# A transformer block for eight batches on one core: the loop over the batches written out, score stacks loaded in halves, maxima taken in the other order

## What is computed

```python
h = layernorm(x) * (1 + ca) + sa
q, k, v = (h @ w.T + (h @ a.T @ b.T) / 16 for w, a, b in three_sets)   # 16 heads of 16
attn = softmax(causal(q @ k.T / 4)) @ v
x = x + ga * lora_linear(attn, wo, ao, bo)
h = layernorm(x) * (1 + cb) + sb
w = top-2 softmax weights of 4 experts, from h @ Wg.T + bg
hid_e = relu(h @ Wi.T + lora_e(h))                                     # 1024 wide, e = 0..3
x = x + gb * sum_e w_e * (hid_e @ Wo.T)
```

## Time and profile of the kernel before

| | |
|---|---|
| time, median of 3 runs | 2154.45 us (2153.02 to 2154.53) |
| span of the profiled execution | 2145.5 us |
| PE busy | 1892.0 us (88%) |
| DVE busy | 1199.8 us (56%) |
| ACT busy | 938.8 us (44%) |
| POOL busy | 529.7 us (25%) |
| mean granted clock of PE | 0.959 |

### The profile page before, as it was taken

The page is one execution under the profiler, slowest core; times in us unless marked ns, Lnnn a source line. Parts: engine busy times, 40 slices in busy tenths (PEclk is TensorE's granted clock), DMA queues, the critical chain, the costliest instruction groups (busy, mean ns, idle before and its releaser), DMA issues.

```text
span 2145.5 us, 36829 instructions
## 1 busy us (share of the span) xinstructions
PE 1892.0 (88%) x11124; PEld 980.5 (46%) x11124; DVE 1199.8 (56%) x2697; ACT 938.8 (44%) x1701; POOL 529.7 (25%) x823
## 2 busy tenths in 40 slices
PE   8687888999889989899889998899898998798858
PEld 5233343455435454354534555354543545344435
DVE  3755567555665557655575556655576554755132
ACT  2254444544444544544444444444445443544421
POOL 3111122322222212223223222222122232132223
PEclk9889989999999999999999999999999999999979
DMA  5523333121433222232331214332222323210100
GB/s 170 80 50 60 60 57 78 22 63 23 80 60 67 33 39 77 31 70 32 65 79 20 62 24 81 60 67 33 36 70 41 70 31 65 31 26 16 35 0 20
DMA packets 72349, 111.82 MB, mean 52 GB/s; under 512 B 13940, under 2 KB 41680, under 8 KB 72152
## 3 DMA queue, kind: packets, MB, share of 16 engines
q1 hardware_dynamic: 72136, 109.31, 27.3%
q10 hardware_dynamic: 16, 0.02, 0.0%
HBM read 75.20 MB, written 33.57 MB: 51 GB/s over the span
## 4 chain that ended last, share of the span: by engine, by line
PE 61%; DVE 14%; DMA 8%; issue 7%; SPq 5%; ACT 4%; POOL 0%; DVEq 0%; POOLq 0%; ACTq 0%
PE mxs L747 11%; PE ov L776 9%; PE st L761 9%; PE dense L856 8%; DMA k_st<-k_parts_scratch 8%; PE dense L841 5%; DVE negm L1147 4%; PE dense L867 4%; PE dense L791 4%; SPq L577 4%; PE dense L833 3%; PE dense L733 3%; PE mxs L751 2%; SPq L581 1%; DVE stats L1018 1%
## 5 line engine op out<-in xcount | busy, mean ns | idle before, releaser
L915 ACT ACTIVATE probs<-st 128x512 f32<-128x512 f32 (+1 forms) x1216 | 666.9, 576 | 651.2 <-PE st L761 613.2
L747 PE MATMUL mxs<-k_st,q_st 96*128 96x512 bf16 (+3 forms) x1536 | 463.4, 333 | 54.6 <-DMA k_st<-k_parts_scratch 48.2
L1147 DVE TENSOR_REDUCE negm<-mxs 128x1 f32<-128x512 f32 (+4 forms) x736 | 416.1, 613 | 147.8 <-PE mxs L751 147.4
L761 PE MATMUL st<-q_st,k_st 98*128 98x512 bf16 (+3 forms) x1536 | 453.0, 335 | 38.9 <-issue 24.3
L1147 DVE TENSOR_REDUCE negm_left<-mxs 128x1 f32<-128x512 f32 x512 | 330.0, 684 | 168.0 <-PE mxs L747 165.5
L776 PE MATMUL ov<-probs,v_g 128*32 128x512 f32 (+3 forms) x3072 | 333.5, 506 | 22.7 <-POOL probs L634 21.9
L747 PEld LDWEIGHTS mxs<-k_st,q_st 96*128 96x128 bf16 x1536 | 149.0, 98 | 333.9 <-issue 101.7
L856 PE MATMUL dense<-c_t,wi_t 128*128 128x512 f32 x512 | 247.3, 605 | 4.3 <-ACT ratio_b L965 3.7
L631 POOL TENSOR_TENSOR fence<-fence 128x1 f32<-128x1 f32 x256 | 49.9, 195 | 756.8 <-ACT probs L915 756.6
L761 PEld LDWEIGHTS st<-q_st,k_st 98*128 98x128 bf16 x1536 | 140.1, 99 | 202.6 <-issue 76.3
L655 POOL TENSOR_TENSOR hid<-hid,second 128x512 f32<-128x512 f32 x128 | 159.8, 1270 | 245.1 <-DVE second L1211 244.6
(11 more groups left out here) (162 smaller groups left out, 1715.3 us busy)
## 6 DMA issues: line engine op xcount, KB each, us to landing
q_st<-q_parts_scratch SPq DMA_DIRECT2D x192, 128.0 KB, 6.9
k_st<-k_parts_scratch SPq DMA_DIRECT2D x192, 128.0 KB, 7.4
q_parts_scratch<-q_part SPq DMA_DIRECT2D x16, 768.0 KB, 3.3
k_parts_scratch<-k_part SPq DMA_DIRECT2D x16, 768.0 KB, 5.4
xin<-in_L_attn_x SPq DMA_DIRECT2D x9, 1024.0 KB, 5.1
x<-in_L_attn_x SPq DMA_DIRECT2D x8, 1024.0 KB, 10.6
out_x<-ob SPq DMA_DIRECT2D x64, 128.0 KB, 1.7
q_st<-m_row SPq DMA_DIRECT2D x128, 4.0 KB
```

Of the source, the lines that this page charges most:

```text
L747: last = nc.tensor.matmul(mxs[:, bank_m, j * n:(j + 1) * n], q_st[0:KS, slot, h0 + j, qt * P:(qt + 1) * P], k_st[0:KS, slot, h0 + j, k0:k0 ...
L761: last = nc.tensor.matmul(st[:, score_bank(ch, kt, h0), j * n:(j + 1) * n], k_st[0:KS + 2, slot, h0 + j, kt * P:(kt + 1) * P], q_st[0:KS + ...
L915: nc.scalar.activation(probs[:, par, h0:h0 + heads, 0:n], st[:, score_bank(ch, kt, h0), 0:heads * n].rearrange("p (j q) -> p j q", q=n), A ...
L1147: nc.vector.tensor_reduce(dst[:, h0:h0 + heads], src, axis=AX.X, op=ALU.max, negate=True).then_inc(max_free, 1)
```

## The change

- `walk` has no loop any more: the six full bodies are written out one after the other, and all waits are on constants.
- `rs` is two steps. The low half (columns 0 to 511 of the stack) is loaded at unit 7, when keys 0 to 511 and queries 0 to 511 of the old group have been scored, the high half at unit 11. Each half is twelve DMAs with runs of 1 KB instead of 2 KB, with a semaphore of its own; maxima of query tiles 0 to 3 wait for the low one alone, tiles 4 to 7 for both. `ps` waits for both halves of both slots.
- `max_steps` runs from tile 0 to tile 7. The maxima of a unit are 3, 4, 4, 4, 4, 5, 5, 5, 5 in every body, now also in unit 0.
- `nm` stands in the middle of unit 9's fillers instead of ahead of them; with one filler it comes behind it. `ce` moves to units 5 and 1, the last group's `ce` and `ct` may start at unit 1, `op` at unit 2.
- In `op` DVE does the addition to x1 as well, behind its own product; POOL has no part of it.
- `relus_covered` moves the next `mx` or `qk` of the same unit between two adjacent `fb`.

```diff
+HALF_READ = (7, NU - 1)
-    for qt in range(7, -1, -1):
+    for qt in range(8):
...
-        put(0, ("ce", GROUPS - 1, 1))
+        put(1, ("ce", GROUPS - 1, 1))
...
-        put(0, *[("ct", i) for i in range(4)])
+        put(1, *[("ct", i) for i in range(4)])
...
-        put(1, *[("op", i) for i in range(4)])
+        put(2, *[("op", i) for i in range(4)])
...
-    row_maxima = [0, 3, 4, 4, 5, 5, 6, 6, 6, 0, 0, 0] if post else [0, 4, 4, 5, 6, 6, 5, 5, 4, 0, 0, 0]
+    row_maxima = [3, 4, 4, 4, 4, 5, 5, 5, 5, 0, 0, 0]
...
-        if k in (4, 0) and u > 0:
-            pinned.append(("ce", g, 0) if k == 4 else ("ce", g - 1, 1))
+        if k in (5, 1) and u > 1:
+            pinned.append(("ce", g, 0) if k == 5 else ("ce", g - 1, 1))
...
-        if k == NU - 1 and (pre or g < 2):
-            plan.append(("rs", g % 2, (g + 2) % GROUPS))
-        fillers.insert(0 if k == NM_UNIT else (len(fillers) + 1) // 2, pinned)
+        if k in HALF_READ and (pre or g < 2):
+            plan.append(("rs", g % 2, HALF_READ.index(k), (g + 2) % GROUPS))
+        fillers.insert((len(fillers) + 1) // 2, pinned)
...
+def relus_covered(steps):
+
+    steps = list(steps)
+    for i in range(len(steps) - 1):
+        if steps[i][0] == steps[i + 1][0] == "fb":
+            near = [j for j in range(i + 2, len(steps)) if steps[j][0] in ("mx", "qk")]
+            if near:
+                steps.insert(i + 1, steps.pop(near[0]))
+    return steps
...
-    plan += pj[0] + [("ps", 0), ("rs", 0, 0), ("rs", 1, 1)]
+    plan += pj[0] + [("ps", 0)] + [("rs", g, half, g) for g in range(2) for half in range(2)]
...
-    with eng.Fori(0, batches - 2) as reg:
-        phase(body_plan(pre=True, post=True, lead=True), reg + 1, reg)
+    for it in range(1, batches - 1):
+        phase(body_plan(pre=True, post=True, lead=True), it)
...
+                    cols = slice(half * HB, (half + 1) * HB)
                     for s in range(SPLIT):
                         for dst, src, part in ((q_st, q_d, Q_PARTS[s]), (k_st, k_d, K_PARTS[s])):
-                            heads = src[ot, rows, part, :].rearrange("(j d) n -> d j n", j=HG)
-                            sp.dma_start(dst[s * DH:(s + 1) * DH, slot, :, :], heads).then_inc(stack_in[slot], 16)
+                            heads = src[ot, rows, part, cols].rearrange("(j d) n -> d j n", j=HG)
+                            sp.dma_start(dst[s * DH:(s + 1) * DH, slot, :, cols],
+                                         heads).then_inc(stack_in[slot][half], 16)
...
-                    pe.wait_ge(stack_in[slot], done(f"rs{slot}") * (2 * SPLIT * 16))
+                    for part in range(1 + qt // 4):
+                        pe.wait_ge(stack_in[slot][part], done(f"rs{slot}{part}") * (2 * SPLIT * 16))
...
                         dve.wait_ge(gates_in, 16 * done("xl"))
+                        dve.wait_ge(x1_in, 16 * done("xl"))
...
+                    dve.wait_ge(dense_free[bank], done(f"bank{bank}") + 1)
+                    nc.vector.tensor_tensor(x1[:, 2 * i:2 * i + 2, :], x1[:, 2 * i:2 * i + 2, :], scaled,
+                                            ALU.add).then_inc(x1_ready, 1)
```

More of the change, by code:

```diff
@@ L190, in body_plan @@
         turns += [((sum(map(pe_cost, together[:i])) + pe_cost(s) / 2) / length, 2, s) for i, s in enumerate(together)]
-        for _, n, s in sorted(turns, key=lambda turn: turn[:2]):
+        for s in relus_covered([s for _, _, s in sorted(turns, key=lambda turn: turn[:2])]):
             plan.append(s)
-            if n == 1 and s is mx[-1] and sum(row_maxima[:k + 1]) == len(max_steps()):
+            if mx and s is mx[-1] and sum(row_maxima[:k + 1]) == len(max_steps()):
                 plan.append(("ms",))
@@ L206, in body_plan @@
     if pre:
-        assert at["vp", 3] < at["vg", 0] and at["ps", 0] < at["rs", 0, 0] and at["ps", 1] < at["rs", 1, 1]
+        assert at["vp", 3] < at["vg", 0] and at["ps", 0] < at["rs", 0, 0, 0] and at["ps", 1] < at["rs", 1, 0, 1]
     return plan
+def relus_covered(steps):
[6 more added lines that the diff above has]
+    return steps
 def hidden_quads(half):
@@ L262, in tallied @@
         names.append("qk diagonal")
-    if step[0] in ("rs", "ps"):
-        names.append(f"{step[0]}{step[1]}")
+    if step[0] == "rs":
+        names.append(f"rs{step[1]}{step[2]}")
+    if step[0] == "ps":
+        names.append(f"ps{step[1]}")
     if step[0] == "w":
@@ L293, in walk, with phase, done @@
     bank_next = [0]
[L295 to L303, removed]
+    def phase(plan, it):
+        steps, bank_next[0] = with_banks(plan, bank_next[0])
         held_back = []
         for s, bank in steps:
-            def done(name, here=dict(here)):
-                fixed = counts.get(name, 0) + here.get(name, 0)
-                return fixed if reg is None or not per.get(name) else reg * per[name] + fixed
+            def done(name, now=dict(counts)):
+                return now.get(name, 0)
             if held_back and s[0] not in ("mx", "pv", "qk"):
@@ L317, in phase @@
             for n in tallied(s, bank):
[L318 to L323, removed]
-    with eng.Fori(0, batches - 2) as reg:
-        phase(body_plan(pre=True, post=True, lead=True), reg + 1, reg)
-    phase(body_plan(pre=False, post=True, lead=False), batches - 1, None)
-    phase(epilogue_plan(), batches, None)
+                counts[n] = counts.get(n, 0) + 1
+    phase(prologue_plan(), -1)
+    phase(body_plan(pre=True, post=False, lead=True), 0)
+    for it in range(1, batches - 1):
+        phase(body_plan(pre=True, post=True, lead=True), it)
+    phase(body_plan(pre=False, post=True, lead=False), batches - 1)
+    phase(epilogue_plan(), batches)
 def after(eng, sem, value):
-    if not isinstance(value, int) or value > 0:
+    if value > 0:
         eng.wait_ge(sem, value)
-def held(eng, value):
-    return value if isinstance(value, int) else eng.to_reg(value)
 def adaln_block(nc, x, wq, aq, bq, wk, ak, bk, wv, av, bv, wo, ao, bo, Wg, bg, Wi, Wo, A, Bm, c, wmod, out):
@@ L494, in adaln_block @@
         part3_ready = sem("part3_ready")
-        stack_in = [sem(f"stack_in{s}") for s in range(2)]
+        stack_in = [[sem(f"stack_in{s}{half}") for half in range(2)] for s in range(2)]
         parts_out = [sem(f"parts_out{i}") for i in range(2)]
@@ L559, in run @@
                     ot = a[0]
-                    stacked = [held(sp, done(f"rs{s}") * (2 * SPLIT * 16)) for s in range(2)]
-                    split = held(sp, done("pj"))
-                    sp.wait_ge(part3_ready, split)
+                    sp.wait_ge(part3_ready, done("pj"))
                     for s in range(2):
-                        after(sp, stack_in[s], stacked[s])
+                        for half in range(2):
+                            after(sp, stack_in[s][half], done(f"rs{s}{half}") * (2 * SPLIT * 16))
                     for dst, src in ((q_d, q_part), (k_d, k_part)):
@@ L643, in run @@
                                             ALU.subtract).then_inc(part3_ready, 1)
[L644 to L651, removed]
                 elif kind == "fb":
```

11 lines of the change are left out of this document (5 added, 6 removed).

## The result

The changed kernel takes 2131.55 us (median; 2128.8 to 2134.77), the kernel before, run beside it, 2153.86 us: a ratio of 0.9897, 95% interval 0.9883 to 0.9911. That is 1% faster. The direction is as forecast, but the gain is 22 us and not 73, and 2131.55 lies above the range, which ended at 2120. The profiled execution took 2129.05 us.

The account below looks back on a forecast made before the run. TensorE was taken to bound most units, VectorE nearly those without fillers. Terms 44 + 52 + 20 - 11 - 39 + 8 - 1 = 73 us off 2145.5 gave 2072.5, with 8.95 added 2081; range 2045 to 2120.

Parts of the forecast that it names:

- maxima spread over nine units: Maxima in all bodies: unit 0 gets some, units with six get five; +8 us gained, bounds 0 to 25.
- The branch: Loop boundaries: writing out five taken branches saves 4.9 us pause and 3.9 half-clock loss each; +44 us, bounds 24 to 48.
- Stack loads: Score-stack waits: early halves land 8 to 9 us after their start; 40 us plus 12 of clock, +52, bounds 25 to 60.
- nm and ce: Waits before nm (groups 2 and 3) and ce shrink as both move later; +20 us, bounds 12 to 26.
- m_row at the end of group 0: m_row loads queue behind two stores on SP, stalling group 1's first score 2.9 us; -11 us, bounds -25 to 0.
- VectorE at the start of group 0: Units 0 to 3: more maxima, norm and x add make TensorE wait 2.3 and 1.3 us; -39, bounds -80 to -10.
- The rest: Small terms: maxima over nine units +8, fb rule 0, batch 0's later stores -2, epilogue's quicker add +1 us.
- The median: Whole kernel: the profiled span's 8.95 us below the runs' median was added, taking 2072.5 to 2081 us.
- (a): Rival, group 0 units 1 to 3: VectorE becomes the bound, 10.6 not 4.6 us a body; 2117 us, chance 0.14.
- (c): Rival, loop boundaries: the stop is arriving code, so straight code stops too and 44 us stay; 2125 us, chance 0.04.
- (d): Rival, groups 0 and 3 of every body: m_row late by 2 us more each; 2105 us, chance 0.07.

Follow-up runs that it names:

- e1: The kernel before with its loop written out and nothing else changed: 2156.89 us, ratio 1.0021 to the kernel before.
- e8: The changed kernel with its six full bodies put back in the loop: 2149.11 us, ratio 0.9988 to the kernel before.
- e7: The changed kernel, without a loop, with both halves of a score stack issued at unit 11: 2202.35 us, ratio 1.0239 to the kernel before.
- e2: The changed kernel with the store of the parts (ps0) moved to unit 11 of group 0, behind nm's loads: 2110.03 us, ratio 0.98.
- e3: The changed kernel with no maxima in unit 0 of group 1, in the full bodies and the last: 2105.84 us, ratio 0.978.
- e4: The changed kernel with the addition to x1 put back on POOL: 2116.9 us, ratio 0.9831 to the kernel before.
- e10: The changed kernel with its six full bodies in the loop and both stack halves issued at unit 11: 2218.45 us in one run.
- e6: The changed kernel with the edits of e2, e3 and e4 together: 2072.91 us, ratio 0.9641 to the kernel before.
- e9: e6 with the first norm's steps (ls1, ln1) issued earlier and group 0's maxima spread differently: 2073.94 us, ratio 0.9634 to the kernel before.

## Why the prediction was wrong in size

Against the 73 us of the sum stand 18.2 us of span, 55 missing. The step that failed is the term "maxima spread over nine units", booked at +8 and measured at -26; with it, m_row was booked at half its size. The branch, booked at 44, is a separate matter: no run gives it that worth. Named in the prediction's own steps:

- **The branch, +44: not a gain of its own.** It was priced as if TensorE's stop were on the path by itself. Taken away alone it is worth 0, because the stack's wait grows by what the stop loses (e1). Taken away last it is worth 17.6 (e8), 26 less than booked, because in the changed kernel the stop and the half clock with it are smaller; why is open. But the idle time booked for the two terms together did go: "issue" and k_st were 72.5 us before and are 2.2 after, 70.3 gone where 64.5 were booked, and none of the 44 us at 1.2 GHz at the five boundaries is left there. Removing one of two waits at the same place brings out the other; removing both gives the sum. How much of the 55 the branch term is short in this change, which does both, depends on what is taken away first, and no run has the early halves without the rest of the change. The price of the clock was somewhat high: half of a stretch at 1.2 GHz is lost only while TensorE works, and it works for 7.44 of 9.1 and 4.91 of 6.2 us.
- **Stack loads, +52: right in mechanism, and in the wait that goes** (46 us for 40 booked); the 12 us of clock in it were not measured by themselves. A half is there after 8.6 us, and 71 us are lost when the early half is taken away (e7). The prediction had also added up the Trainium skill's figure for one transfer of 64 KB ("DMA: Bandwidth & Descriptors", section "Measured") twelve times, an estimate of 11.4 us for a half. That is not borne out for these loads; the measured half decides.
- **nm and ce, +20: about right.** nm's wait fell by 12.1 us (21.8 to 9.7), o_sb's from 13.1 to 0.8. The wait for ctx_n, which belongs to `ct` behind it, fell as well, from 8.9 to 4.2 us.
- **m_row at the end of group 0, -11: right place, half the size.** It measured -21.5 (e2). The step that failed is "m_row (2.43) issued by 854.9": behind the two stores the four issues take 3.88 us, and the wait is 4.39 and not 2.9, which is 9 us in six bodies. The half clock around it is longer than booked, but e2 shows no gain in busy time from it. 10 us of the 55.
- **VectorE at the start of group 0, -39: the walk was right, and it ended too early.** The waits came out as 2.13 and 0.91 for 2.3 and 1.3, and 7.03 in batch 0 for "about 7". But all waits for maxima are 45.6 us in the six full bodies, 7.6 in each where "2 to 4 us a body" were announced; the difference is the 4.39 in group 1. Batch 0's wait:

```profile
94.18 2.70 DVE L1010 BATCH_NORM_STATS2 stats<-xin 128x6 f32<-128x256 f32 x8
...
103.47 0.50 PE L739 MATMUL mxs<-k_st,q_st 96*128 96x384 bf16 x1 [7.03 <-DVE negm L1139]
```

- **The rest, "maxima spread over nine units", +8 (0 to 25): this is the step that failed, and it has the wrong sign.** It looked at what three maxima in unit 0 give TensorE to do and not at what stands ahead of them on VectorE. In group 1 that is the routing chain, 7.9 us, and the cost is 26 us (e3). The walk that was made for group 0 was needed for every group whose unit 0 got maxima. 26 us of the 55 from this and, with the 8 not earned, up to 34. It agrees with where the time was lost, in group 1.
- **The median.** 8.95 us were added between the profiled span and the median of before. After, the median lies 4.25 us above the profiled span (1.75 around it, 2.5 to the median). So 4.7 of the 8.95 belonged to that one execution of the kernel before, and the medians differ by 22.3 us where the spans differ by 18.2. It is no part of the 55.

34 + 10 leave about 11 of the 55 that no run assigns. With the 26 of the branch as e8 counts them the sum would be 70, and other terms would have to have given 15 more than booked; that is not shown. The time at 1.2 GHz moved too: over the prologue and batch 0's body it is 20.4 us where it was 51.2, and TensorE's busy time there is 10.3 us shorter; in the six full bodies it is 106 us where it was 79, and the busy time is 4.5 us longer.

**The rivals.** (a) had the right kind of wait in the wrong group: what was missed is not units 1 to 3 of group 0 but unit 0 of group 1. (c), 2125, is nearest in time, and that is luck: the stop at the boundary is gone from straight code, in e1 and in the changed kernel, and nothing waits for code there. (d) did not occur, since no full body has an m_row wait at the end of group 3. None was the case that came, in which two terms are off in the same direction; the range had let each rival fail alone. The branch's own bounds, 24 to 48, hold neither of its two measured values, 0 and 17.6.

## What to carry to other kernels

A stall that is removed alone is worth only what is left after the next thing that is late at the same place: before it gets a price, look what lies behind it, and run the cheap edit alone (here it was worth 0, and 17.6 us after the other was made). Whenever work is put into a unit that had none, walk the list of the other engine at each of the places, not at the one that looks tightest. And take the wait itself as the worth of removing it, with the clock as an uncertain addition. In the six full bodies the time won was about TensorE's idle time won in e2 (20.7 us for 20.2) and e3 (21.6 for 20.4), and about twice that in e4 (12.4 for 6.6) and at the loop's branches in e8 (19.7 for 8.7).

## What the runs showed of the hardware

- A taken branch costs TensorE a compare-and-branch of 5.9 to 6.6 us in the kernel before and 3.6 to 4.3 in e8 and e10, 0.08 when it falls through; near it single DMA issues of SP take 1.5 to 2.1 us instead of 0.43.
- The four issues that follow two stores of 768 KB on SP took 1.45 us longer than elsewhere (3.88 against 2.43). It is not the m_row loads alone: with nm first, as in the earlier trace rows, the stack's loads behind the stores are the slow ones, 1.24 and 1.09 us instead of 0.43.
- Around the same waits there were 20.4 us at 1.2 GHz in e6 and 30.7 in e9 (epilogue). A difference of 5 us between two kernels can be that alone.
